# Stage 1 of a Hartley-convolution kernel with the image as the stationary operand

## The reference

```python
low_part = jnp.sum(xu * lf, axis=3).reshape(N, C, H, W)
out_low = (low_part * (inside_all + 1.0) - inside_all * gap) * lamb_l[None, :, None, None]
out_high = x * (lamb_h[None, :, None, None] + 1.0)
x = out_low + out_high
...
x_ht = dht_2d(x)
out_ht = out_ht.at[:, :, :M1, :M2].set(compl_mul2d(x_ht[:, :, :M1, :M2], w1))
y = gaussian_smoothing_4d(dht_2d(out_ht) / (H * W))
return y * mask
```

## Time and profile before

| | us |
|---|---|
| median of three runs | 223.38 |
| lowest and highest run | 223.07, 229.33 |
| span of the profiled execution | 224.2 |
| PE busy with matmuls | 184.7 |
| PE's weight loads (beside the matmuls) | 109.8 |
| DVE busy | 143.2 |
| ACT busy | 106.0 |
| POOL busy | 78.5 |

### The profile page before, as it was taken

How to read it: one execution, slowest core, us unless ns; L and a number is a source line. 1 busy time by engine, 2 the same in 40 slices (tenths; PEclk the granted TensorE clock), 3 DMA queues, 4 the chain that set the end, 5 groups by cost and what they waited for, 6 DMA issues and landing times.

```text
span 224.2 us, 3769 instructions
## 1 busy us (share of the span) xinstructions
PE 184.7 (82%) x1274; PEld 109.8 (49%) x1274; DVE 143.2 (64%) x300; ACT 106.0 (47%) x237; POOL 78.5 (35%) x45
## 2 busy tenths in 40 slices
PE   5789995698798999999997999777898988887400
PEld 3136563355354266546564768576555555554200
DVE  0004129999999994862799879908679788753200
ACT  2377750454255233323554210717888888862200
POOL 9970029555767757837476005000000000000000
PEclk9999999589679655556999685999799999999855
DMA  7999999947507506230000000000079999999998
GB/s 192 294 261 311 315 334 337 315 121 196 180 0 194 181 0 187 85 102 0 0 0 1 1 0 0 1 6 0 3 215 280 283 285 282 286 282 281 286 285 234
DMA packets 43792, 37.08 MB, mean 165 GB/s; under 512 B 692, under 2 KB 35676, under 8 KB 43524
## 3 DMA queue, kind: packets, MB, share of 16 engines
q1 hardware_dynamic: 43780, 36.93, 57.3%
HBM read 20.15 MB, written 16.78 MB: 165 GB/s over the span
## 4 chain that ended last, share of the span: by engine, by line
PE 28%; DVE 27%; SPq 12%; ACT 12%; DMA 9%; issue 6%; ACTq 0%; DVEq 0%
ACT modes L572 7%; PE ps L383 6%; SPq L316 5%; PE ps L529 5%; DVE w_acc L829 5%; PE ps L415 5%; DMA w_raw<-mix_w 5%; DVE xht L810 5%; DMA out<-rows 5%; PE ps L393 3%; DVE terms L806 3%; DVE kb_tmp L768 3%; SPq L347 3%; DVE lf_bn L766 3%; PE ps L403 2%
## 5 line engine op out<-in xcount | busy, mean ns | idle before, releaser
L964 POOL TENSOR_TENSOR w_pair<-w_raw 128x640 f32 (+1 forms) x24 | 39.1, 1655 | 28.7 <-DMA w_raw<-mix_w 16.8
L383 PE MATMUL ps<-x_ring,k_wide 128*64 128x512 f32 x128 | 43.3, 762 | 3.3 <-DMA x_ring<-x 3.3
L529 PE MATMUL ps<-cols,k_wide 128*128 128x396 f32 (+2 forms) x96 | 35.3, 505 | 8.8 <-ACT modes L572 4.0
L616 ACT COPY y_sb<-ps 128x448 f32<-128x448 f32 x32 | 29.6, 932 | 21.3 <-PE ps L393 21.3
L611 ACT COPY freq<-ps 128x512 f32<-128x512 f32 x32 | 18.9, 592 | 36.3 <-PE ps L383 36.1
L415 PEld LDWEIGHTS ps<-k_wide,y_sb 128*128 128x128 f32 x192 | 27.9, 224 | 9.4 <-ACT y_sb L616 5.0
L393 PEld LDWEIGHTS ps<-k_wide,freq 128*128 128x128 f32 x128 | 15.9, 160 | 31.4 <-issue 30.2
L572 ACT COPY modes<-x_ring 32x128 f32<-32x128 f32 (+3 forms) x96 | 30.4, 430 | 1.6 <-DVE x_ring L881 0.9
L415 PE MATMUL ps<-k_wide,y_sb 128*128 128x44 f32 x192 | 28.7, 309 | 0.2
L529 PEld LDWEIGHTS ps<-cols,k_wide 128*128 128x128 f32 x96 | 17.2, 196 | 22.0 <-ACT modes L572 8.0
L393 PE MATMUL ps<-k_wide,freq 128*128 128x128 f32 x128 | 25.0, 326 | 0.1
(11 more groups left out here) (68 smaller groups left out, 181.4 us busy)
## 6 DMA issues: line engine op xcount, KB each, us to landing
out<-rows SPq DMA_DIRECT2D x7, 1152.0 KB, 9.4
out<-rows SPq DMA_DIRECT2D x8, 896.0 KB, 8.9
w_raw<-mix_w SPq DMA_DIRECT2D x2, 1200.0 KB, 10.6
out<-rows SPq DMA_DIRECT2D x3, 384.0 KB, 3.2
x_ring<-x SPq DMA_DIRECT2D x2, 512.0 KB, 5.1
k_wide<-wide SPq DMA_DIRECT2D x1, 437.0 KB, 8.5
x_ring<-x SPq DMA_DIRECT2D x15, 0.5 KB, 8.3
k_wide<-wide SPq DMA_DIRECT2D x1, 225.0 KB, 2.7
```

The costliest lines, as they stand in the source:

```text
L383: last = nc.tensor.matmul(ps[half * 64:half * 64 + 64, g % 2, :], const(O_LT, (1, 64)), x_ring[:, u, at:at + G1 // 2 * H], start=True, sto ...
L529: nc.tensor.matmul(ps[:, B_F[k % 3], 0:nt * NW], const(O_LH + s * H, (1, H)), cols[:, u, t:t + nt, :], start=True, stop=True).then_inc(f_d ...
L616: nc.scalar.copy(view(y_sb[:, u, 0, g * G1:g * G1 + 1], (1, G1 // 2), (G1 // 2, 2), (C, NP)), view(ps[:, 2 + g % 2, 0:1], (128, G1 // 2), ...
L964: tt(w_pair[:, k - 1, :, :], lo, hi, ALU.add).then_inc(pairs_done, 1)
```

## The change

Stage 1 swaps its operands. Each channel's image, 128 x 128, is the stationary operand, and the 56 constant columns are streamed. The result of a channel is 128 image columns on partitions by 56 frequencies, which is how `y_sb` wants it. Eight matmuls, one for each channel of a group, fill one PSUM bank at steps of 64 columns; group g uses bank g. The transposes, `freq`, its copy and two semaphores go. The copy into `y_sb` reads the bank with a step of 64 and writes runs of 8 channels. Stage 1 of group g of image n waits for the copy of group g of image n-1. The two keep-busy matmuls ahead of the last stage 2 wait for a copy of the last image, since they write bank 0.

```diff
+                if from_(n, 1):
+                    pe.wait_ge(y_out, n * NG1 + g - 3)
+                for i in range(G1):
+                    at = (g * G1 + i) * H
+                    last = nc.tensor.matmul(ps[:, g, i * 64:i * 64 + NP], x_ring[:, u, at:at + H],
+                                            const(O_LT, (1, NP)), start=True, stop=True)
                 last.then_inc(s1_done, 1)
-
-            def turn_group(n, u, g):
-
-                pe.wait_ge(freq_out, n * NG1 + g + 1)
-                if from_(n, 1) or g >= 2:
-                    pe.wait_ge(y_out, n * NG1 + g - 1)
-                for i in range(G1 // 2):
-                    last = nc.tensor.transpose(ps[:, 2 + g % 2, i * 128:(i + 1) * 128],
-                                               freq[:, g % 2, i * H:(i + 1) * H], const(O_ID, (1, 128)))
-                last.then_inc(turned_y, 1)
...
-            for g in range(NG1 + 1):
-                if g < NG1:
-                    stage1(0, 0, 0, g)
-                if g > 0:
-                    turn_group(0, 0, g - 1)
+            for g in range(NG1):
+                stage1(0, 0, 0, g)
             load_step(1, 0, 1)
...
+            pe.wait_ge(y_out, (N - 1) * NG1 + 1)
             keep_busy(2)
...
-            def keep_freq(n, g):
+            def keep_y(n, u, g):
+
                 act.wait_ge(s1_done, n * NG1 + g + 1)
-                nc.scalar.copy(freq[:, g % 2, :], ps[:, g % 2, :]).then_inc(freq_out, 1)
-
-            def keep_y(n, u, g):
-
-                act.wait_ge(turned_y, n * NG1 + g + 1)
-                nc.scalar.copy(view(y_sb[:, u, 0, g * G1:g * G1 + 1], (1, G1 // 2), (G1 // 2, 2), (C, NP)),
-                               view(ps[:, 2 + g % 2, 0:1], (128, G1 // 2), (64, 2), (1, NP))).then_inc(y_out, 1)
+                nc.scalar.copy(view(y_sb[:, u, 0, g * G1:g * G1 + 1], (C, NP), (1, G1)),
+                               view(ps[:, g, 0:1], (1, NP), (64, G1))).then_inc(y_out, 1)
...
             def load_step(n, u):
-                keep_freq(n, 0)
+                keep_y(n, u, 0)
                 keep_sums(n - 1, 1 - u)
-                keep_freq(n, 1)
-                keep_y(n, u, 0)
-                keep_freq(n, 2)
+                keep_y(n, u, 1)
                 tanh(n - 1)
-                keep_y(n, u, 1)
-                keep_freq(n, 3)
                 keep_y(n, u, 2)
+                keep_y(n, u, 3)
                 keep_data(n - 1, 1 - u)
```

More of the change, by code:

```diff
@@ L232, in hartley_conv_kernel @@
         w_sb = sb("w_sb", [128, S * Q * MODES, C])
-        freq = sb("freq", [128, 2, G1 // 2 * H])
         y_sb = sb("y_sb", [H, 2, NP, C])
@@ L268, in hartley_conv_kernel @@
         x_first, idle_ready = sem("x_first"), sem("idle_ready")
-        freq_out, turned_y = sem("freq_out"), sem("turned_y")
         s1_done, y_out, s2_first, s2_done, pool_done, data_out = map(
@@ L378, in stage1 @@
                     pe.wait_ge(x_in[2 * u + g // 2], it * 16 + 16)
-                if from_(n, 1) or g >= 2:
[L380 to L384, removed]
-                last.then_inc(s1_done, 1)
-            def turn_group(n, u, g):
-                pe.wait_ge(freq_out, n * NG1 + g + 1)
-                if from_(n, 1) or g >= 2:
-                    pe.wait_ge(y_out, n * NG1 + g - 1)
-                for i in range(G1 // 2):
-                    last = nc.tensor.transpose(ps[:, 2 + g % 2, i * 128:(i + 1) * 128],
-                                               freq[:, g % 2, i * H:(i + 1) * H], const(O_ID, (1, 128)))
-                last.then_inc(turned_y, 1)
+                if from_(n, 1):
[4 more added lines that the diff above has]
+                                            const(O_LT, (1, NP)), start=True, stop=True)
+                last.then_inc(s1_done, 1)
             def coefficients(m):
@@ L443, in load_step @@
                 stage1(n, it, u, 1)
-                turn_group(n, u, 0)
                 stage2(n - 1, 1 - u, 1)
@@ L447, in load_step @@
                 stage1(n, it, u, 2)
-                turn_group(n, u, 1)
                 stage2(n - 1, 1 - u, 2)
                 stage1(n, it, u, 3)
-                turn_group(n, u, 2)
                 stage2(n - 1, 1 - u, 3)
                 coefficients(n - 1)
-                turn_group(n, u, 3)
             pe.wait_ge(idle_ready, 1)
@@ L634, in load_step @@
             def load_step(n, u):
-                keep_freq(n, 0)
+                keep_y(n, u, 0)
                 keep_sums(n - 1, 1 - u)
-                keep_freq(n, 1)
-                keep_y(n, u, 0)
-                keep_freq(n, 2)
+                keep_y(n, u, 1)
                 tanh(n - 1)
-                keep_y(n, u, 1)
-                keep_freq(n, 3)
                 keep_y(n, u, 2)
+                keep_y(n, u, 3)
                 keep_data(n - 1, 1 - u)
[L645 to L651, removed]
+            for g in range(NG1):
+                keep_y(0, 0, g)
             act.wait_ge(setup, 1)
```

## The result

The changed kernel takes **285.14 us** (median of four runs, 284.7 to 285.6) against 223.62 for the kernel before (223.07 to 229.33), a ratio of 1.276 with a 95% interval of 1.270 to 1.283. It is slower by 61.5 us. The forecast was 281 us, between 257 and 292. The span of the profiled execution is 283.0 us.

The account below looks back on a forecast made before the run. Before, PE bound the load part at half clock and DVE at full. With PE at half clock, 23.2 us rounds put the last pair at 189.6, 57.7 later: 224.2 + 57.7 = 281.9, less 0.8, 281 us; range 257 to 292.

Parts of the forecast that it names:

- The clock: PE in the load part: 1.2 GHz from the start until the keep-busy batches behind the last coefficients; 80 in 100.
- The witness I named: Granted-clock line: 0.5 from the first matmul to about 190 us; nines in the load part would refute the reading.
- A record of stage 1: New stage-1 matmul record on PE: 0.2125 us at half clock, 0.113 at full, 16 a group, set by the weight load.
- The upper bound, L424's price: Stage-1 record at 0.23 us, as for 82 streamed columns: 0.28 us more a group, 9 us over 32, total 290.
- The round: One image on PE at half clock: stage 1 13.60, stage 2 5.10 and 0.92, filter 0.39, pair 3.17; 23.2 us.
- Behind the last pair: Last terms, mixing and output after the last coefficient pair: everything keeps its length.
- From span to median: Whole kernel: profiled execution lies 0.8 us above the median 223.38, so 281.9 becomes 281 us.
- ScalarE: Copy into y_sb on ACT: 0.5 to 0.93 us, at most 3.7 us a round, off the path and never waited for.
- DVE and GpSimd hidden: Load part: PE's 23.2 us round exceeds DVE's 13.3, so DVE and ACT idle for half of each round.
- The rival at 207 us: Load part at full clock: PE needs 12.2 us a round, DVE's 13.3 sets it; total 207 us; 7 in 100.

Follow-up runs that it names:

- e1_warm: The changed kernel with 12 keep-busy matmuls at its start instead of 3, nothing else: 277.8 us.
- e2_wide: The changed kernel with seven of eight stage-1 matmuls of a group streaming 128 columns instead of 56, the eighth 64: 222.0 us.
- e3_hold: The changed kernel with 8 keep-busy matmuls at the start, one before each stage-1 group of images 1 to 7, three before each coefficient pair: 243.8 us.
- e5_w96: The changed kernel with seven of eight stage-1 matmuls of a group streaming 96 columns instead of 56, the eighth 64: 284.4 us.
- e8_no_pool: The changed kernel with GpSimd's mixing-weight blur after the first share and its sum over images cut to four columns: 285.4 us.
- e7: The changed kernel with seven of eight stage-1 matmuls streaming 128 columns, the eighth 64, and five keep-busy matmuls before each coefficient pair: 220.9 us.

## Why the prediction was right

**The clock: right, and the step that decided.** The forecast was half clock from the first matmul until the keep-busy batch behind the last pair. Stage 1's first 80 records take 22.63 - 5.40 = 17.2 us, 0.215 each, and the trace records the first rise at 200.12, in that batch. The argument (L383 and the transposes stand before a rise, L415-like records before a fall, and the change swaps one for the other) leaned on one rise and one fall. The kernel before has four more falls in the load part, and each stands in or within 2 us behind a wait for kb (40.16, 57.23, 74.30 and 125.50 us); only the one at 132.32 had no such wait, so its rows alone could not part a thin stream from a wait. The experiments do: in e1_warm the new mixture lost the full clock while PE was busy, and in e2_wide a denser stream behind the same loads got it back. That the transposes aren't needed is shown by e2_wide, which has none.

**The witness I named: wrong.** I wrote that nines in the clock line would refute the reading. They came, and the reading stood. What I should have named are durations of unchanged instructions, L402 and L415, at their half-clock values. The rows above held the warning: the first four L383 records, at 5.41 us, take the half-clock 1.98 us under a nine in the clock line.

**A record of stage 1: 0.2125 forecast, 0.215 measured** (46.19 - 42.74 = 3.45 for 16); at full clock 0.113 forecast and 1.8 us for 16 in e1_warm (0.114 each), 1.72 in e3_hold. The formula of the Trainium skill that the prediction quotes (TensorE: Matmul & The Clock Gate, section "LDWEIGHTS (loading the stationary operand)") names no clock; that it holds at both was my reading, and the 0.215 at half clock does not fit it. That the load sets it held up to 128 columns (e2_wide, e5_w96). The upper bound, L424's price, wasn't needed: what makes L424 dearer isn't its 82 columns, since records with 96 cost 3.45 / 16 = 0.216. What does, no run here shows.

**The round: 23.18 forecast, 23.57 measured.** The difference is 0.17 us from the four groups (13.77), 0.11 from L412 (1.03 us against 0.92) and 0.11 from the 24 records of L403 (5.21 against 5.10). Over six rounds that is 2.3 us, and the first pair came at 39.57 instead of 39.0: the last pair at 192.59 instead of 189.6.

**Behind the last pair: 92.4 us kept forecast, 90.4 measured**, which gave 2.0 of these 3.0 us back; this part is unchanged, and why it is shorter I did not look into. That the sum came out within 1.1 us is in part luck: two errors of 3.0 and 2.0 us have opposite signs. The span was forecast at 281.9 and is 283.0.

**From span to median: wrong by 2.6 us.** I took 0.8 us off, since the span of 224.2 lay above the median of 223.38. In the runs listed since, the device time is 1.7 to 2.2 us above its own span (284.81 against 283.0), so the execution profiled before was itself one of some 226 us and not the median one, and 281.9 should have become 283.7.

**ScalarE: right.** The new copy takes 0.532 us, at the lower bound (0.5 to 0.93), and no other engine waits for it. **DVE and GpSimd hidden: right** (e8_no_pool).

**The rival at 207 us was mis-sized.** It took DVE's round from the starts of the pair at 110.34 and 123.63. DVE's own timeline of the kernel before has kb, which the pair waits for, at other times:

```profile
108.08 0.28 DVE L772 TENSOR_TENSOR kb<-kb_tmp,kb_add 40x128 f32<-40x128 f32 x1
...
123.29 0.28 DVE L772 TENSOR_TENSOR kb<-kb_tmp,kb_add 40x128 f32<-40x128 f32 x1
```

From kb to kb are 15.2 us, in which DVE waits at most 0.28 us at a time. The pair at 110.34 started 2.0 us after kb had ended, because PE was late from its half-clock stretch; only the second pair waited for DVE. So the distance of the two starts was too short for DVE's period. The kernel before shows that period between two pairs that both waited for kb:

```profile
57.43 1.64 PE L402 MATMUL ps<-k_narrow,kb 40*128 40x384 f32 x2 [2.19 <-DVE kb L772]
...
73.40 0.91 PE L402 MATMUL ps<-k_narrow,kb 40*128 40x384 f32 x2 [1.45 <-DVE kb L772]
```

They are 16.0 us apart, and the rounds of e2_wide are 15.9. Five of those make 80 us and not 66.5, and the rival would give about 220, no faster than before. e2_wide, which has this rival's clock for most of its time, took 222.0. So my 7 in 100 for faster stood on a period measured between a start that PE delayed and one that DVE delayed: by this estimate even a full clock would have meant no change. By the same token DVE's rounds of 16 us would have covered the change's excess of PE work; the loss of 61 us comes with the clock, as 222.0 us in e2_wide, with the same number of loads, shows.

One slip in the description of the kernel above: the pair L402/L403 writes banks 6 and 7, not 5 and 6. Nothing in the forecast rests on it.

## What to carry to other kernels

Swapping stationary and streamed operands changes not only how many matmuls there are but how many columns stream behind each weight load; where the load sets the pace, as here, extra columns up to the 128 of the load cost nothing, and here they decided which clock the whole stage got. Before removing dense matmuls, look at what stands in the trace just before the clock rose, at every rise and every fall and not at one of each. And take the period of an engine from its own instructions over several rounds, not from the starts of the engine that waits for it.

## What was not expected

- The profile shows full clock where it has no record of one. The changed kernel's mean granted clock is given as 0.98, with 200 us at half clock; e5_w96 is as slow and is given 0.63. Check it with an unchanged instruction.
- A busy PE neither kept the full clock nor got it back: in e1_warm it fell to half and stayed there for 168 us without a gap.
- The width acts as a step: 56 and 96 columns give 285.1 and 284.4 us, 128 give 222.0. Nothing between 96 and 128 was run.
- The kernel before is noisy (218.4 to 229.4 over 11 runs beside e7), the changed one isn't (284.7 to 285.6 over 4). The first crosses between the clocks all through its load part, the second does not, which is the likely reason. Of those 11, the four slowest (227.8 to 229.4) have mean granted clocks of 0.80 to 0.82 and the five from 222.5 to 225.7 have 0.86 to 0.88, but so has the fastest (218.4, 0.87): the clock does not sort them all.
